# Four indirect DMAs at a time: GpSimd waits for each group to land

## What is computed

```python
logits = _gelu(xf @ router_w1 + router_b1) @ router_w2 + router_b2
topk_p, topk_i = jax.lax.top_k(softmax(logits), 2)     # 2 of 8 experts for each token
for _ in range(2):                                      # two iterations
    ctx = concatenate([integrated, v], -1)
    shared_ctrl = _gelu(ctx @ shared_w1 + shared_b1) @ shared_w2 + shared_b2
    ...
    ctrl = _experts(ctx_e, flat_idx, expert_w1, expert_b1, expert_w2, expert_b2)
    ...
    integrated = integrated + halt * (x_next - integrated)
    v = v + halt * (v_next - v)
out = xf + integration_weight * refine(integrated)
```

## Time and profile before

| | |
|---|---|
| runs | 1088.14, 1092.58, 1091.82 us |
| median | 1091.82 us |
| profiled execution, its span | 1104.5 us |
| busy in it | PE 811.1, DVE 656.7, ACT 600.4, POOL 489.7 us |
| indirect DMAs issued by POOL | 96 gathers, 128 scatters, 39 sent back |

### The profile page before, as it was taken

How to read it: one execution, slowest core, us unless ns; L and a number is a source line. 1 busy time by engine, 2 the same in 40 slices (tenths; PEclk the granted TensorE clock), 3 DMA queues, 4 the chain that set the end, 5 groups by cost and what they waited for, 6 DMA issues and landing times.

```text
span 1104.5 us, 13334 instructions
## 1 busy us (share of the span) xinstructions
PE 811.1 (73%) x3968; PEld 567.7 (51%) x3968; DVE 656.7 (59%) x1567; ACT 600.4 (54%) x1064; POOL 489.7 (44%) x436
## 2 busy tenths in 40 slices
PE   7799996778887688979954676735574748775577
PEld 4588884444544466758743454524443524443245
DVE  6532336388778585474804686736564747674556
ACT  5644445444542266576721388725675757675652
POOL 1411112356447734053474445357536654446650
PEclk9899998899999699999975879666697878886879
DMA  9920000000000000000013235636374633533114
GB/s 352 425 34 1 0 1 1 1 0 1 1 1 1 0 1 1 1 1 1 6 53 131 74 86 178 189 104 185 134 234 141 184 119 106 177 110 100 40 57 135
DMA packets 75923, 92.92 MB, mean 84 GB/s; under 512 B 24032, under 2 KB 61920, under 8 KB 73808
## 3 DMA queue, kind: packets, MB, share of 16 engines
q1 hardware_dynamic: 65248, 65.87, 18.7%
q0 software_dynamic: 10464, 25.66, 7.3%
q10 hardware_dynamic: 144, 0.59, 0.2%
HBM read 45.95 MB, written 46.13 MB: 83 GB/s over the span
## 4 chain that ended last, share of the span: by engine, by line
PE 40%; ACT 20%; DVE 19%; issue 13%; another core or an unknown queue 6%; POOL 1%; DMA 0%; DVEq 0%; ACTq 0%; POOLq 0%
PE PS L1958 3%; PE PS L1859 3%; PE PS L1747 3%; PE PS L1941 3%; PE PS L1718 3%; DVE TEMP_R L1131 3%; PE PS L2067 3%; ACT L1565 3%; PE PS L1827 2%; PE PS L1708 2%; ACT KEEP L1522 2%; ACT TEMP_R L1521 2%; PE PS L1661 2%; PE PS L1655 2%
## 5 line engine op out<-in xcount | busy, mean ns | idle before, releaser
L757 POOL DMA_INDIRECT KEEP<-moved,small x96 | 103.8, 1082 | 117.6 <-issue 48.2
L2067 PE MATMUL PS<-TEMP,KEEP 128*128 x320 | 125.7, 537 | 23.2 <-ACT TEMP L1578 20.9
L2087 PE MATMUL PS<-KEEP,TEMP 128*64 128x128 f32 x480 | 47.9, 352 | 112.4 <-issue 53.4
L662 POOL DMA_INDIRECT slots<-KEEP,small x96 | 98.1, 1022 | 57.9 <-issue 27.1
L2087 PEld LDWEIGHTS PS<-KEEP,TEMP 128*64 128x64 f32 x480 | 35.5, 177 | 135.1 <-issue 61.2
L1578 ACT ACTIVATE TEMP<-PS 128x512 f32<-128x512 f32 (+2 forms) x92 | 51.6, 561 | 92.8 <-DVE TEMP L1197 73.1
L1197 DVE COPY TEMP<-PS 128x256 f32<-128x256 f32 (+1 forms) x92 | 44.0, 478 | 95.7 <-remote 63.8
L2067 PEld LDWEIGHTS PS<-TEMP,KEEP 128*128 128x128 f32 x320 | 70.9, 239 | 54.6 <-issue 40.9
L1941 PE MATMUL PS<-TEMP_R 128*128 128x512 f32 x288 | 77.5, 417 | 15.2 <-POOL TEMP_R L702 9.1
L1591 ACT ACTIVATE KEEP<-PS,TEMP 64x128 f32<-64x128 f32 x160 | 57.7, 361 | 54.1 <-remote 44.8
L608 POOL TENSOR_TENSOR KEEP<-KEEP 128x1024 f32<-128x1024 f32 x32 | 63.7, 2005 | 51.7 <-PE PS L1859 49.9
(11 more groups left out here) (272 smaller groups left out, 1948.7 us busy)
## 6 DMA issues: line engine op xcount, KB each, us to landing
slots<-LX SPq DMA_DIRECT2D x14, 1024.0 KB, 25.5
moved<-LX SPq DMA_DIRECT2D x20, 512.0 KB
TEMP<-slots SPq DMA_DIRECT2D x20, 512.0 KB
TEMP<-experts SPq DMA_DIRECT2D x80, 64.5 KB
TEMP<-seconds SPq DMA_DIRECT2D x1, 3072.0 KB, 10.2
TEMP<-early SPq DMA_DIRECT2D x1, 2765.0 KB, 12.0
TEMP<-experts SPq DMA_DIRECT2D x80, 32.5 KB
TEMP<-slots SPq DMA_DIRECT2D x10, 258.0 KB
```

The source lines that it names most:

```text
L662: pool.indirect_dma_start(dst, bass.IndirectOffsetOnAxis(ap=pos[:, h, 2 * m + k:2 * m + k + 1], axis=0), src, None).then_inc(SC[h], 16)
L757: pool.indirect_dma_start(G[:, n % 4, k, 0:w], None, src, bass.IndirectOffsetOnAxis(ap=pos[:, h, 2 * m + k:2 * m + k + 1], axis=0))\
L2067: last = pe.matmul(o, hT[:, e % 3, P * j:P * (j + 1)], EW2[:, 384 * (j % 2):][:, bass.ds(at[j], n)], start=True, stop=True)
L2087: last = pe.matmul(PS[side:side + EHID, bank, part], W1[:, e % 4, j, 1 + EHID * a:1 + EHID * (a + 1)], xTs[:, x % 2, a, part], start=a == ...
```

## The change

POOL gets waits on the semaphores that its own DMAs raise, in program order after each group of at most four. Nothing else is touched. `scattered` waits until the scatters up to tile m have landed, `gathered` until a gather has, `sent` until the slots of a group have arrived in Zd.

```diff
+            def scattered(ph, m):
+
+                h, it = PHASES[ph]
+                pool.wait_ge(SC[h], 32 * (HT * (it - 1) + m + 1))
+
+            def gathered(ph, m):
+
+                n = HT * ph + m
+                pool.wait_ge(GIN[n % 4], 32 * (n // 4 + 1))
+
+            def sent(g):
+
+                pool.wait_ge(BACK[g % 4], sent_back(g % 4, g + 1))
+
             ones_row(0)
             for m in range(HT):
                 scatter(0, m)
+                if m % 2 == 1:
+                    scattered(0, m)
             moved(1)
...
                 for m in range(HT + 4):
                     if m < HT:
                         gather(ph, m)
+                    if m in (1, 3):
+                        gathered(ph, m)
                     if m >= 4:
                         pool.wait_ge(S["v_up"], 2 * (16 * ph + m - 4 + 1))
                         scatter(ph + 2, m - 4)
+                        if m < HT or m % 2:
+                            scattered(ph + 2, m - 4)
             for m in range(4):
                 gather(2, m)
+                if m % 2:
+                    gathered(2, m)
             for s in range(last_group(2) + 1, NG + 2):
                 if s - 2 > last_group(2) and GROUPS[s - 2][0] == "E":
                     slots_back(s - 2)
-                for ph, m in UPDATES.get(s, ()):
-                    if ph == 2 and m + 4 < HT:
-                        gather(2, m + 4)
+                    sent(s - 2)
+                more = [m + 4 for ph, m in UPDATES.get(s, ()) if ph == 2 and m + 4 < HT]
+                for m in more:
+                    gather(2, m)
+                if more:
+                    gathered(2, more[-1])
```

## The result

The changed kernel takes 1104.04 us (median of 4 runs, 1100.24 to 1106.61), the kernel before 1092.20 us on the same chip (4 runs, 1088.14 to 1093.70). The ratio is 1.0111, with a 95% interval of 1.0067 to 1.0155: **slower by 1.1%**. The forecast of 1049 us (1020 to 1098) had the sign wrong.

The account below looks back on a forecast made before the run. It took unbroken bursts of POOL's indirect DMAs to stall the other engines. Terms of -20, -6, -18 and -5 summed to -49, 1104.5 to 1055.5 us; the middle of 1055 and 1043 gave 1049 us, range 1020 to 1098.

Parts of the forecast that it names:

- Bound of the kernel, and the stalls: No engine fills the span; POOL's unbroken DMA bursts over 10 us delay other engines, and pauses of 1.6 to 2 us end this.
- R1: Rival: the pause is too short, stalls stay and waits come on top; 1112 us, chance 0.13.
- R3: Rival: the stalls belong to the recorder, so the waits only cost their 20 us; 1112 us, chance 0.05.
- (a): First scatters: line 1958 falls from some 36 to 7.3 us, part given back at `numbered`; net -20 us.
- What `numbered` gave back: After the first scatters: an unbroken 23 us burst in `numbered` should stall the groups, losing 8 us of the gain.
- (b): Phase 0, first mixed phase: POOL's pace the bound, 110 us instead of 116.3; net -6 us.
- (c): Phase 1, second mixed phase: the same POOL pace gives 110 us instead of 128.8; net -18 us.
- R2: Rival: stalls go, but landings from phase 0 on cost 2.1 us a wait instead of 1.4; some 1080 us, chance 0.15.
- (d): From 951.61 us to the end: 19 waits, 27 us, against unknown pieces of the chain; taken as -5 us.
- The base: Whole kernel: run median 12.7 us under the profiled span, perhaps part of the stalls; the middle of 1055 and 1043 taken.

Follow-up runs that it names:

- e0: The kernel before, unchanged, run and profiled a second time: 1090.22 us, ratio 0.9974, no change.
- e8: Kernel before plus one waited-for memset of a spare tile after each four of the first scatters: 1102.92 us, ratio 0.9995.
- e13: Kernel before plus two waited-for memsets of a spare tile after each four of the first scatters: 1094.94 us, ratio 0.9928.
- e1: Kernel before plus only the change's eight landing waits among the first 32 scatters: 1081.47 us, ratio 0.9863.
- e6: Kernel before plus four waited-for memsets of a spare tile after each four of the first scatters, no landing waits: 1067.52 us, ratio 0.9762.
- e9: Changed kernel with every landing wait replaced by four waited-for memsets of a spare tile: 1079.69 us, ratio 0.9783 to the kernel before.
- e11: Kernel before plus landing waits in the two mixed phases alone, after every eighth DMA: 1083.12 us, ratio 0.9821.
- e12: Kernel before plus four memsets after each four first scatters and after each eighth DMA of the mixed phases, no landing waits: 1066.56 us, ratio 0.9652.
- e3: Kernel before plus only the change's 19 waits of the end (phase 2 gathers, slots sent back): 1106.52 us, ratio 1.0112.
- e2: Kernel before plus only the change's 32 landing waits of the two mixed phases: 1107.38 us, ratio 1.0121.
- e4: Kernel before plus landing waits after every eighth instead of every fourth DMA, first scatters only: 1079.04 us, ratio 0.9858.
- e5: Kernel before plus waits, after each four first scatters, for the four before them, on two semaphores in turn: 1091.70 us, ratio 1.0002.

## Why the prediction was wrong

**Bound of the kernel, and the stalls: right.** They come with unbroken bursts, are in every execution (e0), and a pause ends them. R1 (pause too short) would have needed stalls in the changed kernel; none of over 3 us is left in its chain. What R1 spoke of exists, but at shorter pauses (e8, e13). R3 fell with e1 and e6. The 1112 us of R1 and R3 come nearest to the measured time, but for stalls that stay or never were; that is luck. A slower kernel had been given a chance of 0.17.

**(a) First scatters: right**, -20 forecast, -19.6 by the profile (-21 against e0), 7.3 us for the 64 matmuls. What `numbered` gave back isn't read off by itself. One landing took 7.59 us, so that `moved(1)` came at 603.47 and not at 599.9.

**(b) and (c), the mixed phases: here it failed.** Forecast 110 us each, measured 127.2 and 127.6. The sentence at fault is "From its update to the next phase's gathers are four scatters (5.2 us) and the 11.97 us of idle time". That tail was read from a POOL that waited for v_up, with only the last four scatters behind the last update. With POOL itself as the bound, ten scatters and three waits stand behind the last gather: from its end (912.93) to 941.70 is 28.8 us, where 2 + 17 was put. That is 10 of the 17.6 us by which phase 1 was missed. The rest is the way to the end of the last gather, 98.8 us instead of 91: 6 of these 8 us are the 13 waits, 2.18 us each or 1.88 over the gap, and not 1.4. "POOL's pace is the bound" was right, and its own sum was not carried to the end of POOL's list. R2 had the dearer wait (2.1, nearer than the forecast) but the same short tail, and so came to 1080. Of the 43 us between the forecast span (1055.5) and the measured one (1098.4), 35 lie in (b) and (c).

**The net of (c).** The -18 set a phase of 128.8 us, a fifth of it unknown, against one without stalls. But the stalls had run beside POOL's work, and the 128.8 was that execution's; e0 has 123.1. The patterns of breaks that were tried (e9, e11, e12) took the phase to 117.0 to 119.3: 4 to 6 us under e0, 8 to 10 under the runs on their own chips that left it alone (e8 127.8, e13 127.3), not 18.

**(d) The end: wrong sign.** -5 forecast, +4 by the profile, +9 where it stands alone (e3): POOL makes 34% of the chain there, where it had not been in its first rows.

**The base.** The median was said to be 12.7 us under the span, and half was taken off. e0 shows most of it in the two mixed phases (11.7 us, within their scatter), where the forecast counted it once more as gain.

The Trainium skill ("DMA: Bandwidth & Descriptors", Rules for kernel authors) says to wait late for a DMA. In the mixed phases and at the end that was right, +1.2% and +1.1% (e2, e3). For the first scatters it was not: -1.4% (e1); but e6, which waits for no landing at all, shows that what helped there was the silence and not the wait, so these runs don't speak against the rule. The Trainium skill's fit on the same page (Anatomy of one DMA), 2.0 us plus bytes over 436 GB/s, gives an estimate of 2.15 us for 64 KB; the shortest from issue to the release of POOL's next instruction here is 0.96 + 1.36 = 2.32 us (before `moved(1)`), 2.50 before another DMA, and in the mixed phases mostly 2.7 to 3.4, so the measured numbers decide.

## What to carry to other kernels

When you make one engine's queue slower in order to free the others, write down that queue's whole path to the end of the stage, to the last instruction and to what the next stage needs from it, and compare this with the stage's time; where it is longer, the stalls that you remove cost little. Look for long unbroken runs of POOL's indirect DMAs where PE waits for nobody; break them where POOL has time, after every four with about 1.3 us of silence (after eight, 1.5 us were too little in e12, and landings were enough in e4 and e11), and with something of fixed length rather than a landing. A change that is a loss as a whole may hold a part that is a gain: try its places one by one, and half its density.

## What was not expected of the hardware

- Four memsets of 128x128 between the scatters, 1.0 us of POOL's time for eight times, are worth 2.4% of the kernel (e6), because PE, DVE and SP get on meanwhile. One memset in the same places is worth nothing (e8).
- Waiting instructions that find their value already there change nothing (e5); POOL has to fall silent or slow down.
- While POOL issues, PE gets single matmuls through, 1.4 to 2.8 us apart, without anything in the profile that it waits for.
- Bursts of eight DMAs (10.4 us), each with a landing behind it, are short enough in the first stage (e4).
- A landing can take 7.59 us where 1.54 is usual (578.39 in the changed kernel; 7.11 in e1, 4.54 in e4), in a stretch in which the DMA engines moved 164 GB/s instead of 52, beside SP's load of 3 MB (issued at 568.34); POOL stands still for it.
